# One pair of reciprocal-root operations for two samples, a moved send, and a reordered drain in a three-layer attention and expert kernel

## Chip, cores and metric

One core of one Trainium2 chip. The metric is the device time of one execution in microseconds (us); lower is better. The kernel before was timed three times: median 1148.78 us, from 1148.51 to 1149.47.

## The reference, cut to what matters

The input is 16 samples of 256 tokens with 128 features. Three layers follow one another, each a causal attention with 16 heads of width 8 behind a layer norm:

```
x = x + LN(attn0(LN(x)))                       # phase 0
f = LN(x)
f = f + attn1(LN(f));  h = LN(f)                # phase 1
f = f + token_moe(h)    # each token: its top 2 of 8 experts, gelu FFN 128-512-128
f = f + attn2(LN(f));  h = LN(f)                # phase 2
f = f + seq_moe(h)      # each sample: top 2 of 8 experts, from the mean of h
x = x + LN(f)
```

Each LN here is `(x - mean) / sqrt(var + 1e-5)`, followed by a scale and shift where the layer has one.

## The kernel before, in words

**Items, steps and slots.** A sample in a phase is an item with a number v: v = 0 to 15 is phase 0, 16 to 31 is phase 1 ("phase two" in the name of the change), 32 to 47 is phase 2. The kernel works through a software pipeline by steps n, and each step has four slots k = 0 to 3, one for each group of four heads. In step n the attention scores of item n are made; items n+1 and n+2 (`nxt`, `nxt2`) are prepared; items n-1 to n-5 (`old`, `older`, `oldest`, `first`, and one more) are finished. The order on each engine is written out by hand in one function per engine: `pe_slot`, `act_slot`, `dve_slot`, `pool_slot`, `sp_slot`. A run of such steps covers v = 0 to 31, so that its last steps (n = 32 and on) only finish old items: the drain. Then the token experts run (`pe_jobs` and its fellows), then a second run of steps for v = 32 to 47, then the experts of whole samples.

**The reciprocal roots.** Two layer norms per step need 1/sqrt(var + eps). VectorE (DVE) makes the moments: `post_mv` of item n-2 (`dve_residual_moments`) and `pre_mv` of item n+2, both in slot 2, on either side of the second row-maximum (`dve_reduce`, L616). GpSimd (POOL) makes the roots in `pool_rstd`, an addition (L891) and a power with exponent -0.5 (L893), each over 128 x 2 elements: once for `post_r` at the head of slot 2, and once for `pre_r` between the two causal selects of that slot (`pool_select`, L900). DVE then normalises: `hn` in slot 2 after the third row-maximum (`dve_normalise`, L662), `xn` in slot 3 (L662 too).

**The routed rows.** For each phase-1 item, DVE finds the top two experts of every token (`dve_top`) and the place of each token in its expert's list (`dve_place`, pieces 0 to 5; piece 5, L780, writes the row numbers `x_at`). GpSimd then sends the normalised rows `hk` to `x_routed` in DRAM with four indirect DMAs per item (`pool_send`, L925): send 0 in slot 3 of step v+4, sends 1, 2 and 3 in slots 0, 1 and 2 of step v+5. Piece 5 of item v waits until the sends of item v-2 have landed, because `x_at` has two buffers. Send 0 waits for piece 5 of its item. In slot 3, after its two selects, GpSimd also adds the output bias to `f_all` (`pool_bias`, L953).

**The end of the first run.** When item 31 is counted, `dve_tables` builds the list of expert jobs in 27 small DVE operations, each waiting for the one before; after the 18th (L1093) SyncE and ScalarE write zero padding behind each expert's rows (`pads`, L1359), and SyncE loads the first jobs (L1368) once padding and all sends have landed. TensorE (PE) starts on the jobs when the first rows are there (L1281). `dve_tables` begins by waiting for all seven increments of item 31's placing:

```
dve.wait_ge(placed, NPLACE * B)
```

In `dve_slot` the drain keeps the order of full steps: the normalisation of item n-2 comes ahead of `dve_top(oldest, 0)` (L732).

Of the kernel before, what the change touches and what calls it, by code (L numbers as in the profile page):

```python
# [7 lines left out]
ALU = mybir.AluOpType  # L8
# [7 lines left out]
P = 128  # L16
# [3 lines left out]
NG = H // HG  # L20
E = 8
TOP = 2
EPS = 1e-5
# [9 lines left out]
NPRE, NRSTD, NRES, NSPLIT = 4, 4, 14, 3  # L33
STACK_DMAS = TERMS
NTOP, NPLACE = 5, 7


def need(eng, sem, value):

    if isinstance(value, int) and value <= 0:  # L40
        return
    eng.wait_ge(sem, value)


def build(nc, x_in, w_qk, w_v, w_o, b_qk, b_v, b_o, ln1, ln2, gate_w, gate_b, e_w1, e_b1, e_w2, e_b2, out):
    B, T, D = x_in.shape
# [10 lines left out]
    pe, act, dve, pool, sp = nc.tensor, nc.scalar, nc.vector, nc.gpsimd, nc.sync  # L57

    with ExitStack() as ctx:
        def sb(name, shape, dt=F32):  # L60
            return ctx.enter_context(nc.sbuf_tensor(name, shape, dt))

        def sem(name):
            return ctx.enter_context(nc.semaphore(name))
# [34 lines left out]
        power = sb("power", [P, 2])  # L99
# [3 lines left out]
        pre_mv = sb("pre_mv", [P, 2, 2, 2])  # L103
        pre_r = sb("pre_r", [P, 2, 2])
# [20 lines left out]
        post_mv = sb("post_mv", [P, 2, 2, 2])  # L125
        post_r = sb("post_r", [P, 2, 2])
        st2 = sb("st2", [P, 2, 6])
        mv2 = sb("mv2", [P, 2, 2, 2])
# [68 lines left out]
        res, post_rstd = sem("res"), sem("post_rstd")  # L197
# [486 lines left out]

        def dve_residual_stats(i):
            src = tiles(f_all, i) if i.phase > 0 else [att[:, i.par, j] for j in range(2)]
            dve_stats(src, post_st, res, summed(i))

        def dve_residual_moments(i):
            need(dve, post_rstd, NRSTD * (i.v - 2) + 2)  # L690
            dve_moments(post_st, post_mv[:, i.par], res, summed(i))

        def dve_normalise(i):

            dve.wait_ge(post_rstd, NRSTD * i.v + (2 if i.phase == 0 else NRSTD))
            if i.phase > 0:
                need(dve, hT_ps, i.v - B - 1)
                if i.phase == 1:
                    need(dve, hk_sb, i.v - B - 1)
                dve_normal([hn[:, i.par, j] for j in range(2)], tiles(f_all, i), post_mv[:, i.par],  # L700
                           post_r[:, i.par], res, NRES - 7)
            else:
                att_j = [att[:, i.par, j] for j in range(2)]
                dve_normal(att_j, att_j, post_mv[:, i.par], post_r[:, i.par], res)
# [6 lines left out]
        def dve_f(i):  # L711

            dve.wait_ge(post_rstd, NRSTD * i.v + NRSTD)
            dve_normal(tiles(f_all, i), tiles(x_all, i), mv2[:, i.par], r2[:, i.par], res)
# [104 lines left out]
        def dve_slot(step, k):  # L819
# [51 lines left out]
            if k == 1 and nxt2 and nxt2.phase == 2:  # L871
                dve_combine(nxt2, 1)
            if k == 2 and older:
                dve_normalise(older)
            if k == 2 and ranked:
                dve_top(oldest, 0)
# [4 lines left out]
            if k == 3 and placing:  # L881
                dve_place(first, 5)
            if k == 3 and older and older.phase == 0:
                need(dve, post_rstd, NRSTD * (older.v - 2) + 4)
                dve_moments(st2, mv2[:, older.par], res, NRES * older.v + 8)


        def pool_rstd(mv, r, s, base, last=1):

            alone(pool)  # L890
            nc.gpsimd.tensor_scalar(r, mv[:, :, 1], EPS, None, ALU.add).then_inc(s, 1)  # L891
            pool.wait_ge(s, base + 1)
            nc.gpsimd.tensor_tensor(r, r, power[:], ALU.pow).then_inc(s, last)  # L893
# [62 lines left out]
        def pool_slot(step, k):  # L956
# [4 lines left out]
            if k == 2 and older:  # L961
                pool.wait_ge(res, summed(older) + 4)
                pool_rstd(post_mv[:, older.par], post_r[:, older.par], post_rstd, NRSTD * older.v,
                          1 if older.phase == 0 else NRSTD - 1)
            if k == 0 and oldest and oldest.phase == 0:
                pool.wait_ge(res, NRES * oldest.v + 12)
                pool_rstd(mv2[:, oldest.par], r2[:, oldest.par], post_rstd, NRSTD * oldest.v + 2)
            if ie:
                pool_select(ie, ge, 0)
            if k == 2 and nxt2:  # L970
                pool.wait_ge(pre_stats, NPRE * nxt2.v + 4)
                need(pool, xn_ok, 2 * (nxt2.v - 2) + 2)
                pool_rstd(pre_mv[:, nxt2.par], pre_r[:, nxt2.par], pre_rstd, 2 * nxt2.v)
# [14 lines left out]
            if sending and sending.phase == 1:  # L988
                pool_send(sending, (k + 1) % NG)
# [56 lines left out]
        def dve_tables():  # L1046
# [15 lines left out]
            dve.wait_ge(placed, NPLACE * B)  # L1062
# [17 lines left out]
            step(nc.vector.tensor_reduce(mask, t, AX.X, ALU.add))  # L1080
            step(nc.vector.tensor_tensor(t, t, starts, ALU.mult))
# [17 lines left out]
            flat = [a[:].rearrange("p t r -> p (t r)") for a in (expert_all, place_all, y_at_all)]  # L1099
            step(nc.vector.tensor_copy(t, flat[0].unsqueeze(2).to_broadcast([P, NT * TOP, E])))  # L1100
# [636 lines left out]
```

## Time and profile before

| | |
|---|---|
| median of three runs | 1148.78 us |
| the profiled execution | 1144.85 us, its span 1143.1 us |
| PE busy | 1012.9 us, 89% of the span |
| DVE busy | 875.4 us, 77% |
| ACT (ScalarE) busy | 773.9 us, 68% |
| POOL busy | 703.0 us, 61% |
| GpSimd sends, L925 | 64, mean 1017 ns |
| GpSimd selects, L900 | 384, mean 647 ns |

The span is what the hardware profiler recorded of one execution on the core; the execution's own time is a little longer, since launch and end lie around it. Busy shares are means over stages with different limits. A row of a timeline reads: start in us from the start of the span, duration in us (of all its instructions together, where it ends in x2 or more), engine, line and operation, output and input tile, and in brackets how long the engine was idle before and what released it.

### The profile page before, as it was taken

To read this page: it belongs to the slowest core of one execution; us is meant where nothing else is said; L and a number is where in the kernel's file an instruction comes from. 1 tells how busy PE (TensorE), PEld (TensorE's weight loads), DVE (VectorE), ACT (ScalarE), POOL (GpSimd) and SP (SyncE) were. 2 spreads that over 40 slices of the span, in tenths; PEclk is the share of its full clock that TensorE was granted. 3 is DMA by queue.
4 is the path that set the end of the run, shared out by engine and by line. 5 is a ranking of instruction groups with operands and counts; after the bars stand their busy time and mean duration, and the time that the engine had idled before them with its cause. 6 is when DMAs were issued, how large, how long until landed. Compare 5 with 4: busy or idle time off the path is not lost.

```text
span 1143.1 us, 34934 instructions
## 1 busy us (share of the span) xinstructions
PE 1012.9 (89%) x10453; PEld 789.0 (69%) x10453; DVE 875.4 (77%) x2669; ACT 773.9 (68%) x1913; POOL 703.0 (61%) x1050
## 2 busy tenths in 40 slices
PE   3799999999999999998189999189999999989996
PEld 2566677666677766765189999156666666669986
DVE  5699999999989888887645555178899889856665
ACT  2677777777777777776067778157777777655554
POOL 3466666666667888887623332667888887433331
PEclk8999999999999999999589999589999999999999
DMA  5343212222212222221122222244322222100000
GB/s 159 107 120 82 55 51 56 54 53 56 52 51 63 65 67 67 68 66 37 56 59 70 71 67 63 69 126 124 91 67 70 69 63 61 44 2 15 20 19 24
DMA packets 120711, 73.73 MB, mean 64 GB/s; under 512 B 10736, under 2 KB 115568, under 8 KB 120560
## 3 DMA queue, kind: packets, MB, share of 16 engines
q1 hardware_dynamic: 101552, 51.59, 16.7%
q10 hardware_dynamic: 14912, 11.88, 3.7%
q0 software_dynamic: 4096, 8.40, 2.6%
q8 instruction: 77, 1.26, 0.5%
q14 instruction: 74, 0.61, 0.2%
HBM read 21.68 MB, written 11.60 MB: 29 GB/s over the span
## 4 chain that ended last, share of the span: by engine, by line
PE 31%; DVE 7%; issue 5%; POOL 3%; DMA 3%; ACT 2%; SPq 1%; POOLq 0%; DVEq 0%; ACTq 0%
PE bank L1220 10%; PE bank L1209 9%; DVE wide L616 3%; PE bank L348 2%; DMA stack<-mT 2%; PE bank L393 1%; POOL y_got L944 1%; PE bank L315 1%; PE bank L375 1%; PE bank L334 1%; DVE f_all L795 1%; PE bank L311 1%; ACT prob L503 1%; PE bank L1281 1%; PE bank L381 1%
## 5 line engine op out<-in xcount | busy, mean ns | idle before, releaser
L616 DVE TENSOR_REDUCE wide<-bank 128x2 f32<-128x512 f32 (+1 forms) x576 | 388.7, 678 | 83.7 <-PE bank L307 68.5
L503 ACT ACTIVATE prob<-bank 128x512 f32<-128x512 f32 x576 | 336.8, 592 | 84.8 <-PE bank L329 66.2
L900 POOL TENSOR_SCALAR_AFFINE_SELECT prob<-prob 128x512 f32<-128x512 f32 x384 | 246.1, 647 | 95.5 <-ACT prob L503 93.8
L348 PE MATMUL bank<-prob,vaug 128*32 128x256 f32 (+1 forms) x3072 | 165.3, 333 | 5.2 <-issue 3.9
L1240 POOL COPY w_job<-w_s 128x512 f32 x104 | 66.0, 635 | 154.2 <-PE bank L1209 153.5
L315 PE MATMUL bank<-stack 126*128 126x256 bf16 x768 | 147.8, 273 | 0.0
L334 PE MATMUL bank<-stack 128*128 128x256 bf16 x768 | 146.8, 272 | 0.9 <-ACT prob L503 0.9
L1220 PE MATMUL bank<-w_job,prob 128*128 128x128 f32 x1088 | 139.0, 276 | 1.9 <-issue 1.6
L1231 ACT ACTIVATE prob<-bank,b_job 128x128 f32<-128x128 f32 (+1 forms) x416 | 132.0, 400 | 8.6 <-PE bank L1209 7.8
L348 PEld LDWEIGHTS bank<-prob,vaug 128*32 128x32 f32 x3072 | 81.5, 109 | 78.6 <-issue 46.6
L1220 PEld LDWEIGHTS bank<-w_job,prob 128*128 128x128 f32 x1088 | 131.3, 192 | 5.5 <-issue 4.5
L311 PE MATMUL bank<-maskneg,identb 128*128 128x256 bf16 x384 | 105.7, 275 | 5.5 <-DVE wide L616 4.6
L329 PE MATMUL bank<-stack 128*128 128x128 bf16 x768 | 75.1, 220 | 19.3 <-DMA stack<-mT 18.3
L514 ACT COPY mT<-bank 8x256 bf16<-8x256 bf16 x192 | 67.8, 353 | 33.3 <-PE bank L359 33.1
L925 POOL DMA_INDIRECT x_routed<-hk,x_at x64 | 65.1, 1017 | 28.0 <-DVE x_at L780 11.1
L334 PEld LDWEIGHTS bank<-stack 128*128 128x128 bf16 x768 | 73.3, 97 | 12.4 <-ACT prob L503 1.8
L315 PEld LDWEIGHTS bank<-stack 126*128 126x128 bf16 x768 | 75.8, 99 | 6.4 <-issue 0.6
L305 PE MATMUL bank<-maskneg,identb 128*128 128x512 bf16 x192 | 74.0, 385 | 6.1 <-DMA stack<-parts 4.6
L944 POOL DMA_INDIRECT y_got<-y_routed,y_at x64 | 63.8, 997 | 25.0 <-POOL y_at L941 12.2
L1209 PE MATMUL bank<-oT,w_job 128*128 128x128 f32 x576 | 77.5, 278 | 0.0
L307 PEld LDWEIGHTS bank<-stack 126*128 126x128 bf16 x768 | 59.9, 98 | 24.8 <-issue 1.1
L625 DVE TENSOR_TENSOR wide<-wide 128x8 bf16<-128x8 f32 x192 | 71.6, 373 | 6.6
(186 smaller groups left out, 2029.4 us busy)
## 6 DMA issues: line engine op xcount, KB each, us to landing
stack<-parts SPq DMA_DIRECT2D x576, 64.0 KB
w_s<-e_w ACTq DMA_DIRECT2D x32, 256.0 KB, 3.1
oT<-x_routed SPq DMA_DIRECT2D x72, 64.0 KB, 1.8
y_routed<-oT SPq DMA_DIRECT2D x36, 128.0 KB, 1.9
stack<-mT SPq DMA_DIRECT2D x192, 4.0 KB
out<-x_all SPq DMA_DIRECT2D x16, 128.0 KB, 1.8
b_all<-e_b ACTq DMA_DIRECT2D x2, 512.0 KB, 4.0
x_routed<-hk,x_at POOLq DMA_INDIRECT x64, 2.3
```

The source lines that it names most:

```text
L311: nc.tensor.matmul(o[:, :, P:T], identb[:], maskneg[:, 0:2], start=True, stop=False, skip_group_check=True)
L315: m = nc.tensor.matmul(o[:, h], q[:, hh, P:T], k[:, hh, :], start=False, stop=True, skip_group_check=True)
L329: m = nc.tensor.matmul(bk[:, h * P:(h + 1) * P], k[:, p0 + h, P:T], q[:, p0 + h, P:T], start=True, stop=True)
L334: m = nc.tensor.matmul(bk[:, h * T:(h + 1) * T], k[:, hh, 0:P], q[:, hh, :], start=True, stop=True)
L348: m = nc.tensor.matmul(o, w, (prob0, prob1)[kb][:, g % 2, h], start=kb == 0, stop=kb == 1, skip_group_check=True)
L503: nc.scalar.activation(o, s, ACT.Exp, scale=SCALE).then_inc(exp_done, 1)
L616: nc.vector.tensor_reduce(o, s, AX.X, ALU.max, negate=True).then_inc(max_done, 1)
L900: nc.gpsimd.affine_select(out=t, in_=t, compare_op=ALU.is_ge, fill=0.0, base=0, pattern=[[0, HG], [1, P]], channel_multiplier=-1).then_inc ...
L944: nc.gpsimd.indirect_dma_start(y_got[:, i.par, t, rank], None, y_routed, bass.IndirectOffsetOnAxis(ap=y_at[:, i.par, t, rank:rank + 1], ax ...
L1209: m = nc.tensor.matmul(bank[2 * par + c // 2][:, (c % 2) * T:(c % 2) * T + width], w1_job[:, par, c * P:(c + 1) * P], rows, start=True, st ...
L1220: m = nc.tensor.matmul(y_bank[par][:, t * P:(t + 1) * P], hid[:, par, c, t * P:(t + 1) * P], w2_job[:, par, c], start=(c == 0), stop=(c == ...
L1231: nc.scalar.activation(hid[:, par, c, 0:width], bank[2 * par + c // 2][:, (c % 2) * T:(c % 2) * T + width], ACT.Gelu, bias=b1_job[:, par, ...
```

## The change

Three edits:

- **Roots of two samples together.** For items v with 16 <= v < 28 (`joint`), the roots of item n-2 (`post_r`) and item n+2 (`pre_r`) are one addition and one power over 128 x 4 elements, at the head of slot 2, once both moments are there; the pair between the two selects is gone. That holds for steps n = 18 to 29. The tiles `pre_mv`, `post_mv` and `pre_r`, `post_r` become halves of common tiles, `power` has four columns. The semaphores are counted anew (`post_ready`, `x_rstd`).
- **Sends.** While `nxt2` exists (n < 30 in the first run), send 2 moves from slot 1 to slot 2, where send 3 follows it. After that the sends keep their slots.
- **Drain.** In steps without a current item `dve_top(oldest, 0)` comes ahead of `dve_normalise(older)`. `dve_tables` waits only for the counts (piece 2) of item 31; piece 5 of item 31 moves from slot 3 into the tables, behind their eighth operation (L1080).

```diff
-        power = sb("power", [P, 2])
+        power = sb("power", [P, 4])
-        pre_mv = sb("pre_mv", [P, 2, 2, 2])
-        pre_r = sb("pre_r", [P, 2, 2])
+        pre_post_mv, pre_post_r = sb("pre_post_mv", [P, 2, 2, 2, 2]), sb("pre_post_r", [P, 2, 2, 2])
+        (pre_mv, post_mv), (pre_r, post_r) = ([a[:, :, kind] for kind in range(2)] for a in (pre_post_mv, pre_post_r))
...
+        def joint(v):
+            return B <= v and v + 4 < 2 * B
+        separate = [v for v in range(3 * B) if not joint(v)]
+        def post_ready(v):
+            return (pre_rstd, 2 * (v + 4) + 2) if joint(v) else (post_rstd, 2 * separate.index(v) + 2)
...
         def dve_normalise(i):
-            dve.wait_ge(post_rstd, NRSTD * i.v + (2 if i.phase == 0 else NRSTD))
+            dve.wait_ge(*post_ready(i.v))
...
+            if k == 2 and ranked and not cur:
+                dve_top(oldest, 0)
             if k == 2 and older:
                 dve_normalise(older)
-            if k == 2 and ranked:
+            if k == 2 and ranked and cur:
                 dve_top(oldest, 0)
...
-            if k == 3 and placing:
+            if k == 3 and placing and first.v < 2 * B - 1:
                 dve_place(first, 5)
...
-        def pool_rstd(mv, r, s, base, last=1):
+        def pool_rstd(mv, r, s, base):
...
-            nc.gpsimd.tensor_tensor(r, r, power[:], ALU.pow).then_inc(s, last)
+            exponents = power[:, 0:2] if len(r.shape) == 2 else power[:].rearrange("p (a b) -> p a b", a=2)
+            nc.gpsimd.tensor_tensor(r, r, exponents, ALU.pow).then_inc(s, 1)
+        def pool_pre(i, mv, r):
+            pool.wait_ge(pre_stats, NPRE * i.v + 4)
+            need(pool, xn_ok, 2 * (i.v - 2) + 2)
+            pool_rstd(mv[:, i.par], r[:, i.par], pre_rstd, 2 * i.v)
...
             if k == 2 and older:
                 pool.wait_ge(res, summed(older) + 4)
-                pool_rstd(post_mv[:, older.par], post_r[:, older.par], post_rstd, NRSTD * older.v,
-                          1 if older.phase == 0 else NRSTD - 1)
+                if joint(older.v):
+                    pool_pre(nxt2, pre_post_mv, pre_post_r)
+                else:
+                    pool_rstd(post_mv[:, older.par], post_r[:, older.par], post_rstd, post_ready(older.v)[1] - 2)
...
-            if k == 2 and nxt2:
-                pool.wait_ge(pre_stats, NPRE * nxt2.v + 4)
-                need(pool, xn_ok, 2 * (nxt2.v - 2) + 2)
-                pool_rstd(pre_mv[:, nxt2.par], pre_r[:, nxt2.par], pre_rstd, 2 * nxt2.v)
+            if k == 2 and nxt2 and not (older and joint(older.v)):
+                pool_pre(nxt2, pre_mv, pre_r)
...
             if sending and sending.phase == 1:
-                pool_send(sending, (k + 1) % NG)
+                for n in (((1,), (2,), (3,), (0,)) if not nxt2 else ((1,), (), (2, 3), (0,)))[k]:
+                    pool_send(sending, n)
...
         def dve_tables():
-            dve.wait_ge(placed, NPLACE * B)
+            dve.wait_ge(placed, NPLACE * B - NPLACE + 4)
...
             step(nc.vector.tensor_reduce(mask, t, AX.X, ALU.add))
+            dve_place(Item(2 * B - 1, 1, 1), 5)
             step(nc.vector.tensor_tensor(t, t, starts, ALU.mult))
...
+            dve.wait_ge(placed, NPLACE * B)
             step(nc.vector.tensor_copy(t, flat[0].unsqueeze(2).to_broadcast([P, NT * TOP, E])))
```

## Rows read from the trace of the kernel before

**Rows 1.** Busy time in a stretch of phase 1: PE, PEld, DVE, ACT, POOL, clock, DMA share, GB/s

```profile
410.00:451.00 41.00, 39.21 (x450) 28.38 (x449) 36.52 (x125) 30.78 (x71) 35.52 (x53) 1.00 0.25 68
```

**Rows 2.** Waits of PE from 343 to 510 us: total, times, longest

```profile
PE bank L400 <- DVE on L635: 3.6, 9, 0.4
```

**Rows 3.** Timeline of POOL in step 22, end of slot 1 to slot 3

```profile
377.52 0.98 POOL L925 DMA_INDIRECT x_routed<-hk,x_at  x1 [0.15 <-issue]
378.54 0.24 POOL L891 TENSOR_SCALAR post_r<-post_mv 128x2 f32<-128x2 f32 x1
378.94 0.72 POOL L893 TENSOR_TENSOR post_r<-post_r,power 128x2 f32<-128x2 f32 x1 [0.15 <-POOL post_r L891]
...
380.25 0.21 POOL L891 TENSOR_SCALAR pre_r<-pre_mv 128x2 f32<-128x2 f32 x1
380.54 0.71 POOL L893 TENSOR_TENSOR pre_r<-pre_r,power 128x2 f32<-128x2 f32 x1
...
382.02 1.11 POOL L925 DMA_INDIRECT x_routed<-hk,x_at  x1 [0.17 <-issue]
...
384.35 0.72 POOL L953 TENSOR_TENSOR f_all<-f_all,bo_s 128x256 f32<-128x256 f32 x1
```

**Rows 4.** Timeline of DVE in the same step

```profile
378.28 0.24 DVE L651 BATCH_NORM_AGGREGATE pre_mv<-pre_st 128x2 f32<-128x6 f32 x2
...
379.70 0.91 DVE L662 TENSOR_SCALAR hn<-f_all,post_mv,post_r 128x128 f32<-128x128 f32 x2 [0.31 <-POOL post_r L893]
...
384.58 0.53 DVE L625 TENSOR_TENSOR wide<-wide 128x8 bf16<-128x8 f32 x1
```

**Rows 5.** Timeline of PE: the stall after step 22 and after step 30

```profile
386.63 0.44 PE L400 MATMUL bank<-ident,on 128*128 128x128 f32 x2 [0.39 <-DVE on L635]
...
519.23 0.44 PE L400 MATMUL bank<-ident,on 128*128 128x128 f32 x2 [0.90 <-DVE on L635]
```

**Rows 6.** Timeline of POOL in step 30: two selects in a row, and the bias

```profile
512.83 1.21 POOL L900 TENSOR_SCALAR_AFFINE_SELECT prob<-prob 128x512 f32<-128x512 f32 x2
...
517.03 0.73 POOL L953 TENSOR_TENSOR f_all<-f_all,bo_s 128x256 f32<-128x256 f32 x1
```

**Rows 7.** Timeline of DVE in step 30

```profile
512.88 1.24 DVE L662 TENSOR_SCALAR hn<-f_all,post_mv,post_r 128x128 f32<-128x128 f32 x2 [0.83 <-POOL post_r L893]
```

**Rows 8.** Timeline of DVE in step 20: moments that an idle POOL waits for

```profile
344.42 0.23 DVE L651 BATCH_NORM_AGGREGATE post_mv<-post_st 128x2 f32<-128x6 f32 x2
```

**Rows 9.** Timeline of POOL in step 20

```profile
344.85 0.22 POOL L891 TENSOR_SCALAR post_r<-post_mv 128x2 f32<-128x2 f32 x1 [0.84 <-DVE post_mv L651]
```

**Rows 10.** Groups of POOL instructions by shape, whole execution: busy us, mean ns

```profile
L909 POOL TENSOR_TENSOR rest<-qkf,parts 128x512 f32<-128x512 f32 x48 | 55.8, 1163 | 18.6 <-ACT parts L524 14.9 <-issue 0.4
...
L953 POOL TENSOR_TENSOR f_all<-f_all,bo_s 128x256 f32<-128x256 f32 x32 | 23.2, 725 | 0.0
```

**Rows 11.** Timeline of DVE in the drain

```profile
549.12 0.60 DVE L662 TENSOR_SCALAR hn<-f_all,post_mv,post_r 128x128 f32<-128x128 f32 x2 [1.43 <-POOL post_r L893]
549.63 0.23 DVE L732 MAX8 mx_all<-lgt 128x8 f32<-128x8 f32 x2
...
555.83 0.19 DVE L776 TENSOR_REDUCE place_all<-picked 128x4 f32<-128x32 f32 x1
558.29 0.16 DVE L780 SCALAR_TENSOR_TENSOR x_at<-expert_all,place_all 128x4 uint32<-128x4 f32 x1 [2.28 <-DMA x_routed<-hk,x_at]
...
562.12 0.76 DVE L1081 TENSOR_TENSOR prob<-prob,js 128x576 f32<-128x576 f32 x1
```

**Rows 12.** Timeline of POOL in the drain: a send right behind another, and the last

```profile
546.98 0.96 POOL L925 DMA_INDIRECT x_routed<-hk,x_at  x1 [0.30 <-issue]
...
566.88 1.14 POOL L925 DMA_INDIRECT x_routed<-hk,x_at  x1 [0.30 <-issue]
```

**Rows 13.** The chain of waits, in order of time: landing of sends, padding, first job

```profile
555.92 2.27 DMA x_routed<-hk,x_at
...
570.09 1.74 DMA x_routed<-zeros
```

More of the change, by code:

```diff
@@ L32 @@
 SPREAD = 4
-NPRE, NRSTD, NRES, NSPLIT = 4, 4, 14, 3
+NPRE, NRES, NSPLIT = 4, 14, 3
 STACK_DMAS = TERMS
@@ L124, in build @@
         post_st = sb("post_st", [P, 2, 6])
-        post_mv = sb("post_mv", [P, 2, 2, 2])
-        post_r = sb("post_r", [P, 2, 2])
         st2 = sb("st2", [P, 2, 6])
@@ L196, in build @@
         o1_ps, attn_n, o2_ps, onT_sb, o3_ps = sem("o1_ps"), sem("attn_n"), sem("o2_ps"), sem("onT_sb"), sem("o3_ps")
-        res, post_rstd = sem("res"), sem("post_rstd")
+        res, post_rstd, x_rstd = sem("res"), sem("post_rstd"), sem("x_rstd")
         hT_ps, hT_sb, lg_ps, lg_sb = sem("hT_ps"), sem("hT_sb"), sem("lg_ps"), sem("lg_sb")
@@ L689, in dve_residual_moments @@
         def dve_residual_moments(i):
-            need(dve, post_rstd, NRSTD * (i.v - 2) + 2)
+            if i.v >= 2:
+                dve.wait_ge(*post_ready(i.v - 2))
             dve_moments(post_st, post_mv[:, i.par], res, summed(i))
         def dve_normalise(i):
-            dve.wait_ge(post_rstd, NRSTD * i.v + (2 if i.phase == 0 else NRSTD))
+            dve.wait_ge(*post_ready(i.v))
             if i.phase > 0:
@@ L711, in dve_f @@
         def dve_f(i):
-            dve.wait_ge(post_rstd, NRSTD * i.v + NRSTD)
+            dve.wait_ge(x_rstd, 2 * i.v + 2)
             dve_normal(tiles(f_all, i), tiles(x_all, i), mv2[:, i.par], r2[:, i.par], res)
@@ L880, in dve_slot @@
                 dve_place(first, 4)
-            if k == 3 and placing:
+            if k == 3 and placing and first.v < 2 * B - 1:
                 dve_place(first, 5)
             if k == 3 and older and older.phase == 0:
-                need(dve, post_rstd, NRSTD * (older.v - 2) + 4)
+                need(dve, x_rstd, 2 * (older.v - 2) + 2)
                 dve_moments(st2, mv2[:, older.par], res, NRES * older.v + 8)
-        def pool_rstd(mv, r, s, base, last=1):
+        def pool_rstd(mv, r, s, base):
             alone(pool)
-            nc.gpsimd.tensor_scalar(r, mv[:, :, 1], EPS, None, ALU.add).then_inc(s, 1)
+            nc.gpsimd.tensor_scalar(r, mv[..., 1], EPS, None, ALU.add).then_inc(s, 1)
             pool.wait_ge(s, base + 1)
-            nc.gpsimd.tensor_tensor(r, r, power[:], ALU.pow).then_inc(s, last)
+            exponents = power[:, 0:2] if len(r.shape) == 2 else power[:].rearrange("p (a b) -> p a b", a=2)
[4 more added lines that the diff above has]
+            pool_rstd(mv[:, i.par], r[:, i.par], pre_rstd, 2 * i.v)
         def pool_select(i, g, u):
@@ L962, in pool_slot @@
                 pool.wait_ge(res, summed(older) + 4)
-                pool_rstd(post_mv[:, older.par], post_r[:, older.par], post_rstd, NRSTD * older.v,
-                          1 if older.phase == 0 else NRSTD - 1)
+                if joint(older.v):
+                    pool_pre(nxt2, pre_post_mv, pre_post_r)
+                else:
+                    pool_rstd(post_mv[:, older.par], post_r[:, older.par], post_rstd, post_ready(older.v)[1] - 2)
             if k == 0 and oldest and oldest.phase == 0:
                 pool.wait_ge(res, NRES * oldest.v + 12)
-                pool_rstd(mv2[:, oldest.par], r2[:, oldest.par], post_rstd, NRSTD * oldest.v + 2)
+                pool_rstd(mv2[:, oldest.par], r2[:, oldest.par], x_rstd, 2 * oldest.v)
             if ie:
                 pool_select(ie, ge, 0)
-            if k == 2 and nxt2:
-                pool.wait_ge(pre_stats, NPRE * nxt2.v + 4)
-                need(pool, xn_ok, 2 * (nxt2.v - 2) + 2)
-                pool_rstd(pre_mv[:, nxt2.par], pre_r[:, nxt2.par], pre_rstd, 2 * nxt2.v)
+            if k == 2 and nxt2 and not (older and joint(older.v)):
+                pool_pre(nxt2, pre_mv, pre_r)
             if k == 1 and nxt:
```

## Prediction

> **What bounds the kernel now.** First the busy time by stretch. In phase 1 PE is busy 39.21 of 41 us at full clock [rows 1]: it bounds these steps, and only time in which it stands still can be won. Then PE's waits there: they put nine stalls, 3.6 us together, ahead of the transposes of L400, each waiting for DVE's `on` [rows 2]; one of them is the 0.39 us at 386.63 [rows 5]. The count fits steps 21 to 29, the joint steps in which sends run. A step takes about 16.6 us there (519.23 less 386.63, over eight steps [rows 5]).
>
> Then the timelines, to see who makes DVE late. In slot 2 DVE idles 0.31 us for `post_r` ahead of `hn` [rows 4], which comes late because send 2 sits ahead of it on GpSimd and ends where L891 starts [rows 3]. But this is not yet what sets PE's stall. In slot 3 DVE's L625, over 8 elements, takes 0.53 us and ends at 385.11, just after GpSimd's bias (384.35 and 0.72, to 385.07) [rows 3, 4]: it is held until the bias is done. From the bias's end to L400 is 1.56 us in this step. In step 30 the bias ends at 517.76 and L400 starts at 519.23, 1.47 us later [rows 5, 6], though DVE had idled 0.83 us for its roots there [rows 7]. So the chain is GpSimd up to its bias, then DVE, then PE, and **what counts is when GpSimd ends its slot 3**, not how long DVE waits in slot 2.
>
> At the end of the first run another chain holds: sends of item 29 land, piece 5 of item 31, the tables, the padding, the first job [rows 11, 13].
>
> **Part 1, one pair of roots (12 steps).** It removes the second pair: 0.21 and 0.71 us, from 380.25 to 381.25, less 0.03 by which the next select overlaps: -0.97 us of GpSimd [rows 3]. The joint pair must wait for `pre_mv`, which ends at 378.52 [rows 4]. An idle GpSimd starts 0.20 us after such moments (344.65 to 344.85) [rows 8, 9], so at 378.72 instead of 378.54 [rows 3]: +0.18 us. DVE's wait ahead of `hn` gets no shorter by that, it grows to about 0.5 us. Behind the pair the two selects now follow one another, as in step 30, where the two operations of `hn`, begun beside them, took 1.24 us [rows 6, 7] against 0.91 us now [rows 4]; in exchange `xn` has no select beside it. Both lie in DVE's time before it is held by the bias, so I cost them at nothing; if that cover goes they are worth about 0.3 us each way.
>
> No row shows a power over four elements. Below, it costs as much as over two (+0). Above, all that the power adds doubles: L909 over 512 elements takes 1163 ns and L953 over 256 takes 725 [rows 10], which extrapolates to some 0.29 us for a very small two-input operation, so of 0.72 us [rows 3] 0.43 us belong to two powers, and two more cost +0.43. I take +0.2, about the middle, since no row lies nearer to either end. A gain is excluded: it is the same operation on more data.
>
> The Trainium skill (GPSIMD Engine Reference, section 3.1) puts two-input GpSimd operations at about 2.6 cycles for each element of a partition, by which two more elements would be nearly free. The power row, with its 0.43 us over the extrapolated add, speaks for a dearer element; by the page alone the term would be 0, which is a rival below.
>
> **Part 2, the send.** Send 2 leaves slot 1 (0.98 us [rows 3]). That frees nothing: GpSimd would be waiting for `pre_mv` there anyway, since the send ends at 378.50. In slot 2 it comes behind the selects and send 3 follows it: one send of 0.98 us [rows 3] and the 0.30 us that lies between two sends in a row [rows 12], +1.28 us. The send there now takes 1.11 us [rows 3], beside `xn`; up to 0.1 us may come back.
>
> Sum for GpSimd's slot 3: +0.18 - 0.97 + 1.28 = +0.49, less 0.1, so **+0.4 us, and +0.6 with the power**. It passes the selects of slot 3, the bias, L625, `x_at`, `on` and L400, whose stall grows from 0.4 to about 1.0 us. Send 0 waits for `x_at` and moves with it. Nine steps: +5.4 us. In steps 18 to 20 no send runs in slot 2, the pair removed outweighs the later start, and GpSimd comes to slot 3 before its data: 0. Steps 30 and 31 are unchanged.
>
> **Part 3, the drain.** `x_at` of item 31 waits 2.28 us for the sends of item 29, and the tables start right behind it, at about 558.5; the operation ahead of it ends at 556.02 [rows 11]. The tables can start then: -2.45 us. Their ninth operation starts at 562.12, 3.6 us after the first [rows 11], so piece 5 in its new place comes at about 559.7, later than the landing at 558.19 [rows 13], so it waits no more and costs its own 0.2 us: +0.2. `dve_top` moved ahead lies in DVE's idle time (1.43 us before `hn`), and the most of its 0.23 us leaves the chain, in step 32 and again in step 33 [rows 11]; I estimate that 0.15 us of it reaches the tables, since from step 34 TensorE's and ScalarE's work on the last item's `hn` leads. Together **-2.4 us**.
>
> What is late next: the last send starts at 566.88 [rows 12] and a send lands 2.27 us after its start [rows 13], at 569.15, some 0.3 us sooner with the drain's earlier start. The padding lands at 571.83 [rows 13], and -2.4 makes it 569.4. So the gain just fits; the sends are 0.2 to 0.6 us behind taking over.
>
> **Sum.** +5.4 - 2.4 = **+3.0 us**. The profiled execution took 1144.85 us (span 1143.1), 3.9 us below the median of 1148.78; I add to the median: **1151.8 us**. A difference of 0.2%, 2.3 us, is about what a measurement of this kernel can tell from no change.
>
> **Rivals.**
> - *The power over four costs no more than over two* (or the send gives more back). Then nine steps cost 9 x 0.4 = 3.6 us, less 2.4: **+1.2, 1150.0 us**, no change. For it: an addition over 2 elements takes 0.21 to 0.24 us [rows 3], so most of a small operation is fixed. Against: the power's 0.43 us above.
> - *Faster: DVE gets past the bias.* With `xn` free of a select (about 0.3 us sooner) L625 may start before GpSimd's later bias does. It decides if DVE reaches L625 after the last select and before the bias; then GpSimd is no longer ahead of `on`, DVE's own queue is, and the stall of 0.39 us shrinks by some 0.2: -1.8 - 2.4 = **-4.2, 1144.6 us**. Against: in step 30 the interval from bias to L400 held although DVE stood otherwise, and the next small operations would be held in L625's place.
> - *The drain gives nothing*, because indirect sends beside the earlier tables run longer (1.14 us against 0.96 [rows 12]) and land last, with those of item 31 behind a later `x_at`. Then **+5.4, 1154.2 us**. Against: `x_at` comes at 559.9, its send in about 563.
>
> The Trainium skill (SBUF — State Buffer, "Who interferes with whom") says that a fast-mode VectorE copy or scalar operation and GpSimd lock one another out of a port pair, descriptor writing included. Of that the send of 1.11 us beside `xn` shows 0.13 us; by the rule two sends beside `xn` could be held by up to its whole length, which would lie on the slower side of my sum.
>
> **How the numbers follow.** Forecast 0.44, power free 0.26, DVE past the bias 0.22, drain gives nothing 0.08. With the power at its upper bound the forecast ends at 9 x 0.83 - 2.4 = +5.1. Low end 1144.5 (the faster rival), high end 1154.3. Forecast's own range: 1150 to 1154; a sixth of it is below +2.3. Slower: 0.37 + 0.08 = 0.45; same: 0.26 + 0.07 = 0.33; faster 0.22.
>
> **What would show it.** Right: steps 21 to 29 at about 17.2 us; L400's wait some 1.0 us each, still 1.5 us behind the bias's end; `hn` pairs of 1.2 us behind a wait of 0.5 to 0.7; the power over 128x4 at about 0.9 us; the tables' first operation some 2.5 us sooner after item 31's last `hn`; the padding still landing last. Wrong: a power at 0.72 (rival one), L400's wait at 0.4 or less with L625 short again (rival two), SyncE's first job waiting for a send (rival three).

## The result, and the profile after

The changed kernel takes **1152.96 us** (median of 11 runs, 1150.23 to 1156.62); the kernel before, run beside it, 1148.51 us (11 runs, 1144.83 to 1150.14). The ratio is 1.0043, 95% interval 1.0031 to 1.0055: slower by 4.9 us, between 3.6 and 6.3. The forecast was 1151.8 us, 3.0 above its base, in a range of 1144.5 to 1154.3.

The profiled execution of the changed kernel took 1156.49 us, span 1154.8, so it was one of its longest; its span is 11.7 us above the one of before. Not all of that is the change: of the 11.5 us by which its last GpSimd `rest` (L927; L909 before) is late, 2.3 were there before the first joint step and 2.3 more come in the middle of the second run, where nothing was changed. (The other traces stand there, ahead of the first joint step, between 0.9 us ahead and 2.7 behind; and all four traces of the third occasion below, e10 and e11 without joint roots among them, show the same long step of about 19 us in the second run.) So the steps are read from this profile and, where ends matter, from a second profile of the same kernel (run `e8_changed_again`, span 1146.7 us), in which `rest` stood 0.1 us *ahead* of before when the joint steps began. Lines have moved: L393 is now L391, L400 L398, L616 L614, L625 L623, L635 L633, L651 L649, L662 L660, L780 L789, L891 and L893 are L902 and L905, L900 L918, L925 L943, L953 L971, L1281 L1302, L1359 L1380. In e3 and e4 GpSimd's lines stand two lower (L903, L916, L969).

The page's busy time, to set beside the table of before: every engine is as busy as it was, or less.

```profile
PE 1012.7 (88%) x10358; PEld 789.7 (68%) x10453; DVE 869.9 (75%) x2669; ACT 774.0 (67%) x1913; POOL 698.6 (60%) x1026
```

Phase 1 by stretch, as in [rows 1] (PE, PEld, DVE, ACT, POOL, clock, DMA share, GB/s). GpSimd is busy 2.9 us less in it. The same clock times cut the steps elsewhere, though; over eight whole steps, from `rest` to `rest` (377.79 to 515.65; before 373.62 to 506.80), it is 108.76 us for 113.75, 0.62 less a step. And yet the steps are longer:

```profile
410.00:451.00 41.00, 38.92 (x445) 27.77 (x446) 34.61 (x114) 30.29 (x72) 32.62 (x43) 1.00 0.23 65
```

Next the timeline of GpSimd over slots 2 and 3 of a joint step, to be read against [rows 3]:

```profile
417.33 0.23 POOL L902 TENSOR_SCALAR pre_post_r<-pre_post_mv 128x4 f32<-128x4 f32 x1 [1.33 <-DVE pre_post_mv L649]
417.64 1.05 POOL L905 TENSOR_TENSOR pre_post_r<-pre_post_r,power 128x4 f32<-128x4 f32 x1
418.68 1.22 POOL L918 TENSOR_SCALAR_AFFINE_SELECT prob<-prob 128x512 f32<-128x512 f32 x2
420.08 1.09 POOL L943 DMA_INDIRECT x_routed<-hk,x_at  x1 [0.18 <-issue]
421.47 0.96 POOL L943 DMA_INDIRECT x_routed<-hk,x_at  x1 [0.30 <-issue]
422.45 1.23 POOL L918 TENSOR_SCALAR_AFFINE_SELECT prob<-prob 128x512 f32<-128x512 f32 x2
423.64 0.72 POOL L971 TENSOR_TENSOR f_all<-f_all,bo_s 128x256 f32<-128x256 f32 x1
```

And DVE in the same stretch, against [rows 4]:

```profile
416.90 0.24 DVE L649 BATCH_NORM_AGGREGATE pre_post_mv<-pre_st 128x2 f32<-128x6 f32 x2
...
418.73 1.25 DVE L660 TENSOR_SCALAR hn<-f_all,pre_post_mv,pre_post_r 128x128 f32<-128x128 f32 x2 [0.72 <-POOL pre_post_r L905]
...
420.63 0.62 DVE L660 TENSOR_SCALAR xn<-f_all,pre_post_mv,pre_post_r 128x128 f32<-128x128 f32 x2
...
423.35 0.40 DVE L623 TENSOR_TENSOR wide<-wide 128x8 bf16<-128x8 f32 x1
423.67 0.73 DVE L750 CAST expert_all<-mi 128x4 f32<-128x4 uint32 x1
```

The joint addition starts 0.19 us behind the second moments (417.14 to 417.33). The power takes 1.05 us, `hn` waits 0.72 us and then takes 1.25, `xn` only 0.62. Two sends stand behind the two selects, 0.30 us apart. The bias ends at 424.36, which is 7.22 us after the moments of `pre_mv`; before it was 6.55 (378.52 to 385.07 [rows 3, 4]): 0.67 us later. DVE's cast L750 ends with it, at 424.40, then come the row numbers and `on`, and PE's L398 starts at 425.84:

```profile
425.84 0.44 PE L398 MATMUL bank<-ident,on 128*128 128x128 f32 x2
```

Where PE stands still for it differs from one execution to the next. In the second profile it waits at L398 in all nine steps; in the profile of the result at L398 for DVE in two only, and in five ahead of L373, for ScalarE's `xT` (1.2 us), though its steps are as long. First the second profile, PE's waits from 343 to 515 us (total, times, longest), against [rows 2]:

```profile
PE bank L398 <- DVE on L633: 4.5, 9, 0.5
PE bank L309 <- DVE wide L614: 3.0, 10, 0.3
PE bank L391 <- ACT oT L507: 2.7, 10, 0.3
```

Two of PE's transposes there, seven steps apart:

```profile
388.98 0.44 PE L398 MATMUL bank<-ident,on 128*128 128x128 f32 x2 [0.51 <-DVE on L633]
...
509.51 0.44 PE L398 MATMUL bank<-ident,on 128*128 128x128 f32 x2 [0.50 <-DVE on L633]
```

A step takes 120.53 / 7 = **17.22 us**; before it was 16.65 from one `rest` to the next (132.60 / 8 = 16.58 by [rows 5], which take in step 30). The old stall grew only from 0.4 to 0.5 us. The same count in the profile of the result:

```profile
PE bank L398 <- DVE on L633: 0.7, 2, 0.4
```

The second wait is new: ten times 0.3 us ahead of L309, the matmul of the mask, released by a row maximum of DVE (L614), in both profiles. This stall is already there in the first joint steps, where the old one was not and no send runs in slot 2 (PE, profile of the result):

```profile
336.01 0.28 PE L309 MATMUL bank<-maskneg,identb 128*128 128x256 bf16 x1 [0.29 <-DVE wide L614]
...
352.49 0.28 PE L309 MATMUL bank<-maskneg,identb 128*128 128x256 bf16 x1 [0.30 <-DVE wide L614]
...
420.77 0.28 PE L309 MATMUL bank<-maskneg,identb 128*128 128x256 bf16 x1 [0.30 <-DVE wide L614]
```

Over exactly those steps the windows show PE idle 8.39 us of seven steps, 1.20 each; in the kernel before, from 386.63 to 519.23, 132.60 - 126.24 = 6.36 us of eight, 0.80 each:

```profile
388.98:509.51 120.53, 112.14 (x1260) 80.45 (x1275) 103.50 (x337) 88.95 (x205) 95.07 (x127) 1.00 0.23 64
```

That would be 0.40 of the 0.6 us, as much as 0.1 at L398 and 0.3 at L309. But this count is rough, since some matmul records are missing: e1 below, whose steps are those of the kernel before, shows 1.00 us of idle a step over six steps. So PE's idle time doesn't say how much is lost where.

What does is the distance from the end of `pre_mv`'s moments (L649) to the start of L398, in us, in the settled steps, where it repeats within some 0.02 us from step to step. The kernels e3 to e9 are those of the experiments below:

| kernel | `pre_mv` to end of bias | `pre_mv` to L398 | step | step less `pre_mv` to L398 |
|---|---|---|---|---|
| before | 6.55 | 8.11 | 16.65 | 8.54 |
| e3 joint roots only | 6.59 | 8.19 | 16.73 | 8.54 |
| e4 moved send only | 6.87 | 8.05 | 16.59 | 8.54 |
| e9 send and drain | 6.89 | 8.06 | 16.60 | 8.54 |
| the change (result) | 7.22 | 8.70 | 17.23 | 8.53 |
| the change (e8) | 7.20 | 8.68 | 17.22 | 8.54 |
| e6 change, bias late | 9.84 | 8.07 | 16.67 | 8.60 |
| e7 send, drain, bias late | 9.36 | 7.58 | 16.20 | 8.62 |

All that the step gains or loses lies between these two points (the last column stays within 0.1; e10 has 8.01 and 8.48, e11 8.17 and 8.60), also in the profile in which PE hardly waits at L398. In the change the bias ends 0.65 to 0.67 us later, and L398 comes 0.57 to 0.59 later with it.

The drain's timeline of DVE in that profile: the tables begin at 561.99, and piece 5 of item 31 follows 3.5 us later without a wait; before it had waited 2.28 us, ahead of the tables [rows 11].

```profile
561.99 0.28 DVE L1084 COPY prob<-counts 128x256 f32<-128x256 f32 x1
...
565.50 0.16 DVE L789 SCALAR_TENSOR_TENSOR x_at<-expert_all,place_all 128x4 uint32<-128x4 f32 x1
```

At the 32nd `rest`, behind the last of the joint steps, it was 6.35 us behind before; its tables start 3.50 us later, its first job 3.64 us later (578.67 against 575.03). So the drain gives back 2.7 us there. What the first job now waits for is the last send. The chain of waits, in order of time, against [rows 13], and SyncE's padding beside it, issued from 570.14 to 573.79:

```profile
572.95 2.53 DMA x_routed<-hk,x_at
...
577.84 1.93 DMA oT<-x_routed
```

```profile
570.14 3.65 SPq L1380 DMA_DIRECT2D x_routed<-zeros  x4
```

In the profile of the result it is otherwise. It is 8.85 us behind at the 32nd `rest` and 6.31 at the tables (564.80), 2.5 less, but 8.71 at the first job (583.74): only 0.1 us is given back. The paddings took longer, and the last of them landed at 580.46, behind the sends, of which the last started at 574.51:

```profile
573.49 5.77 SPq L1380 DMA_DIRECT2D x_routed<-zeros  x4
```

### The profile page after: what moved, and what is told of

Same layout as the page of the kernel before. It is cut to its first block, busy times and chain, and to the rows that moved or that the text cites. A ratio compares the mean times of both kernels' runs of the same rounds, so it can differ in the third digit from the quotient of the medians.

```text
span 1154.8 us, 34784 instructions
## 1 busy us (share of the span) xinstructions
PE 1012.7 (88%) x10358; PEld 789.7 (68%) x10453; DVE 869.9 (75%) x2669; ACT 774.0 (67%) x1913; POOL 698.6 (60%) x1026
## 4 chain that ended last, share of the span: by engine, by line
PE 59%; DVE 12%; issue 11%; DMA 7%; POOL 5%; ACT 4%; SPq 1%; DVEq 0%; POOLq 0%; ACTq 0%
PE bank L1241 10%; PE bank L1230 9%; PE bank L346 8%; DMA stack<-mT 5%; PE bank L313 4%; DVE wide L614 4%; PE bank L332 4%; PE bank L373 3%; PE bank L391 3%; PE bank L305 2%; PE bank L309 2%; PE bank L404 2%; PE bank L327 2%; PE bank L365 2%; PE bank L379 1%
## 5 line engine op out<-in xcount | busy, mean ns | idle before, releaser
L614 DVE TENSOR_REDUCE wide<-bank 128x2 f32<-128x512 f32 (+1 forms) x576 | 389.0, 679 | 94.8 <-PE bank L305 70.3
L918 POOL TENSOR_SCALAR_AFFINE_SELECT prob<-prob 128x512 f32<-128x512 f32 x384 | 246.4, 649 | 99.1 <-ACT prob L501 97.1
L309 PE MATMUL bank<-maskneg,identb 128*128 128x256 bf16 x384 | 106.2, 277 | 11.7 <-DVE wide L614 10.8
L305 PE MATMUL bank<-stack 126*128 126x128 bf16 x768 | 75.1, 220 | 10.8 <-DMA stack<-parts 3.6
L943 POOL DMA_INDIRECT x_routed<-hk,x_at x64 | 64.7, 1012 | 28.1 <-issue 10.9
L507 ACT COPY oT<-bank 128x256 f32<-128x256 f32 x192 | 69.8, 364 | 7.4 <-PE bank L346 6.1
```

Source lines behind the costliest of these rows:

```text
L305: m = nc.tensor.matmul(o[:, h], q[:, p0 + h, 0:P], k[:, p0 + h, 0:P], start=False, stop=True, skip_group_check=True)
L309: nc.tensor.matmul(o[:, :, P:T], identb[:], maskneg[:, 0:2], start=True, stop=False, skip_group_check=True)
L614: nc.vector.tensor_reduce(o, s, AX.X, ALU.max, negate=True).then_inc(max_done, 1)
L918: nc.gpsimd.affine_select(out=t, in_=t, compare_op=ALU.is_ge, fill=0.0, base=0, pattern=[[0, HG], [1, P]], channel_multiplier=-1).then_inc ...
```

## The experiments

All kernels compute the full result. Each was timed in five rounds beside the kernel before. They ran on three occasions (the first and the third on one chip, the second on another), on which the kernel before took 1144.62 us (24 runs), 1145.48 (17) and 1148.62 (31); ratios are compared within an occasion first. The ratio stands with its 95% interval. The step is the mean of the last six before the drain, from one `rest` to the next; in the kernel before it is 16.65 us.

| run | occasion | median us | ratio to before | step us |
|---|---|---|---|---|
| e1 drain only | 1 | 1140.95 | 0.9970 [0.9955, 0.9985] | 16.61 |
| e2 steps only | 1 | 1150.61 | 1.0045 [1.0032, 1.0059] | 17.24 |
| e3 joint roots only | 1 | 1148.45 | 1.0031 [1.0018, 1.0043] | 16.73 |
| e4 moved send only | 1 | 1143.18 | 0.9981 [0.9967, 0.9995] | 16.59 |
| e8 the change again | 2 | 1150.55 | 1.0043 [1.0028, 1.0058] | 17.22 |
| e9 send and drain | 2 | 1142.02 | 0.9963 [0.9948, 0.9977] | 16.60 |
| e6 change, bias late | 2 | 1147.38 | 1.0016 [1.0002, 1.0030] | 16.67 |
| e7 send, drain, bias late | 2 | 1139.54 | 0.9945 [0.9927, 0.9962] | 16.20 |
| e12 the change, third time | 3 | 1151.98 | 1.0033 [1.0020, 1.0047] | 17.23 |
| e13 steps only again | 3 | 1154.35 | 1.0050 [1.0034, 1.0067] | 17.24 |
| e10 as e7, first run only | 3 | 1146.46 | 0.9982 [0.9966, 0.9997] | 16.49 |
| e11 as e10, send in slot 1 | 3 | 1148.55 | 0.9998 [0.9983, 1.0014] | 16.77 |

**The halves of the change.** Steps and drain taken apart. The edits are to the changed kernel. e1 takes back joint roots and send:

```diff
-            return B <= v and v + 4 < 2 * B
+            return False
...
-                for n in (((1,), (2,), (3,), (0,)) if not nxt2 else ((1,), (), (2, 3), (0,)))[k]:
+                for n in ((1,), (2,), (3,), (0,))[k]:
```

> The drain's edits alone; roots and sends as before. Theory: the tables start 2.5 us sooner behind the last steps, padding and first job come 2.4 us sooner, ratio to before 0.998. Rival: the padding beside the last sends is issued more slowly (5.7 us for SyncE's four instead of 3.6, as the profile of the changed kernel shows), so the tables are sooner by 2.6 us and the first job by under 0.5 us; ratio 1.000. Steps 21 to 29 stay at 16.65 us in both.

e2 takes back the drain, and e13 is the same kernel once more:

```diff
-            if k == 2 and ranked and not cur:
-                dve_top(oldest, 0)
...
-            if k == 2 and ranked and cur:
+            if k == 2 and ranked:
...
-            if k == 3 and placing and first.v < 2 * B - 1:
+            if k == 3 and placing:
...
-            dve.wait_ge(placed, NPLACE * B - NPLACE + 4)
+            dve.wait_ge(placed, NPLACE * B)
...
-            dve_place(Item(2 * B - 1, 1, 1), 5)
```

> Joint roots and moved send, drain as before. Theory: steps 21 to 29 take 17.2 us, the time rises by 5.5 to 7 us, ratio 1.005 to 1.006. Rival (the loss is from the new places of the tiles or is disturbance, since the profile also shows 1.5 us more near the start and 2.3 us near the end): steps at 16.65 to 16.8, ratio under 1.002.

The drain alone is 3.4 us faster by its ratio (1.7 to 5.2). In its trace the tables start at 556.20, before at 558.49, behind steps that are 0.3 us late by then, so 2.6 us sooner. The first job is 2.6 us sooner on the same count. In its chain of waits the last send comes last:

```profile
567.18 2.52 DMA x_routed<-hk,x_at
...
572.07 1.98 DMA oT<-x_routed
```

The steps alone are 5.2 us slower (3.7 to 6.8), with PE's waits as in the second profile of the change, to a tenth (L398 4.6 us in 9, L309 3.0 in 10). So the loss is in the steps, and the drain by itself does what it was forecast to do.

**The two edits of the steps apart.** e3 and e4 keep the old drain. e3 leaves the sends where they were (the second edit of e1), e4 keeps two pairs of roots (the first edit of e1).

> Joint roots, send 2 still in slot 1, drain as before. Theory (the end of GpSimd's bias in slot 3 sets the step): GpSimd loses the second pair (0.97 us) and adds 0.17 for the later start and 0.33 for the larger power, so the bias ends 0.5 us sooner than before, the steps take 16.5 to 16.7 us, change between -1.5 and +1 us, though VectorE waits 0.7 to 0.9 us for the roots. Rival (VectorE's wait ahead of hn sets the step): steps at 17.1 us or more, +4 to +6 us.

> Two sends in slot 2, separate roots, drain as before. Theory (bias): the bias ends about 0.35 us later than before, steps at about 17.0 us, +3 us, although VectorE no longer waits for its roots ahead of hn. Rival (VectorE's wait ahead of hn sets the step): that wait of 0.31 us is gone, steps at 16.35 us, -2.8 us.

Neither alone lengthens the settled step: +0.08 us with the joint roots, -0.06 with the moved send, **+0.58 with both**. The parts don't add up. The prediction had priced them as a bundle: it charged the moved send in full because, with joint roots, GpSimd would wait for `pre_mv` in the time that leaving slot 1 frees.

With the joint roots alone PE's waits from 343 to 515 us are only these. The 0.4 us at L400 are gone, and the 0.3 at L309 have taken their place:

```profile
PE bank L309 <- DVE wide L614: 3.0, 10, 0.3
PE bank L391 <- ACT oT L507: 2.7, 10, 0.3
```

DVE and GpSimd in e3: `hn` waits 0.84 us, and DVE comes to L623 at 422.55, when the bias, begun at 421.96, is all but over. Nothing is held. But the bias isn't 0.5 us sooner, as I had expected: it ends 6.59 us after `pre_mv`, before 6.55. GpSimd now waits for ScalarE's `prob` ahead of its selects (from 395 to 497 us 4.9 us in 12 waits, of a kind that doesn't stand among its waits before), so what it saved with the second pair is lost again; and DVE, late by `hn`, reaches L398's `on` no sooner either:

```profile
417.80 1.25 DVE L660 TENSOR_SCALAR hn<-f_all,pre_post_mv,pre_post_r 128x128 f32<-128x128 f32 x2 [0.84 <-POOL pre_post_r L903]
...
422.55 0.17 DVE L623 TENSOR_TENSOR wide<-wide 128x8 bf16<-128x8 f32 x1
422.67 0.17 DVE L750 CAST expert_all<-mi 128x4 f32<-128x4 uint32 x1
```

```profile
421.96 0.73 POOL L969 TENSOR_TENSOR f_all<-f_all,bo_s 128x256 f32<-128x256 f32 x1
```

The ratio of e3, 1.0031, is more than 0.08 us a step makes: its first four joint steps lose 1.7 us, so that the trace accounts for 2.3 of the 3.5 us (2.1 to 4.9). I had expected +1 us at most: the settled steps were as expected, the first four were not.

With the moved send alone the bias is late, as I expected of this run: it ends 0.3 us later against its step than before. But `hn` waits for nothing now, since no send stands ahead of its roots:

```profile
415.80 0.17 DVE L623 TENSOR_TENSOR wide<-wide 128x8 bf16<-128x8 f32 x1
415.92 1.32 DVE L750 CAST expert_all<-mi 128x4 f32<-128x4 uint32 x1
417.15 0.17 DVE L785 TENSOR_REDUCE place_all<-picked 128x4 f32<-128x32 f32 x1
417.36 0.52 DVE L789 SCALAR_TENSOR_TENSOR x_at<-expert_all,place_all 128x4 uint32<-128x4 f32 x1
...
428.37 0.60 DVE L660 TENSOR_SCALAR hn<-f_all,pre_post_mv,pre_post_r 128x128 f32<-128x128 f32 x2
```

```profile
415.92 1.24 POOL L916 TENSOR_SCALAR_AFFINE_SELECT prob<-prob 128x512 f32<-128x512 f32 x2
417.11 0.73 POOL L969 TENSOR_TENSOR f_all<-f_all,bo_s 128x256 f32<-128x256 f32 x1
```

DVE is early enough that L623 runs before the selects, the cast is held to their end (417.24 against 417.16) and L785 runs beside the bias. Only `x_at` is held to the bias's end, 417.88 against 417.84. So fewer operations are left behind the bias, and from its end to L398 it is 1.18 us, not 1.5: L398 comes 8.06 us after `pre_mv` as against 8.11 before. My rule "L400 is 1.5 us behind the bias" expected a slower kernel here; it is 2.2 us faster by its ratio (0.6 to 3.8). In its trace the first job comes 1.5 us sooner (573.56 against 575.03), of which 0.4 us was there before the first joint step. PE still waits at L398, and longer than before, since it gets there sooner:

```profile
PE bank L398 <- DVE on L633: 5.0, 9, 0.6
```

So the stall of L398 does not measure the loss: 0.40 us a step before, 0.56 here, 0.50 in the change, none in e3. The rule held in the changed kernel (424.36 to 425.84 is 1.48) only because DVE stands there as it did in steps 22 and 30.

**Is it the bias?** If the loss needs both a late DVE and a late bias, moving the bias behind send 0 and the copy of `hk` in slot 3 must take it away with both edits in. e8 is the changed kernel as it is, beside it. e9 takes the joint roots alone back out of the change (the first edit of e1). e6 is the changed kernel with

```diff
-            if k == 3 and nxt and nxt.phase > 0:
-                pool_bias(nxt)
...
                 nc.gpsimd.tensor_copy(hk[:, oldest.par], hn[:, oldest.par]).then_inc(hk_sb, 1)
+            if k == 3 and nxt and nxt.phase > 0:
+                pool_bias(nxt)
```

> The changed kernel itself, once more beside the others. Theory (the profile of it had a disturbed padding): SyncE's four paddings take 3.64 us as everywhere else, the first job comes about 6.3 - 2.6 = 3.7 us later than before, ratio about 1.003. Rival (roots, moved send and new drain together always lose the drain's gain): paddings take 5 us or more again, ratio 1.0045 or more. Steps 21 to 29 at 17.24 us in both.

> The changed kernel with GpSimd's bias moved behind send 0 and the copy of hk in slot 3. Theory (in the combination it is the bias that holds VectorE's row numbers, and the late hn is covered as in the kernel with joint roots alone): x_at is written about 0.5 us sooner, steps fall from 17.24 to 16.7 to 16.9 us, 3 to 5 us less than the changed kernel. Rival (the late hn and xn themselves set the step): steps stay at 17.1 us or more.

> The moved send and the new drain without the joint roots. If the parts add up: 0.9981 x 0.997, about -5 us, ratio 0.995 to 0.996. Rival (the drain's gain is taken by the sends, which here end at the same distance behind the steps): ratio 0.998. Steps at 16.55 to 16.6 us.

With the late bias the step goes from 17.22 to 16.67 us, `x_at` is written 6.90 us after `pre_mv` instead of 7.52 (e8), PE's waits at L398 vanish (9 times 0.5 in e8, none here) and L309 keeps its 2.9 us. An L623 of the next slot is now held, to the end of the two selects behind the bias (424.72 against 424.69), but PE waits nowhere for it:

```profile
422.80 0.73 POOL L971 TENSOR_TENSOR f_all<-f_all,bo_s 128x256 f32<-128x256 f32 x1
423.48 1.21 POOL L918 TENSOR_SCALAR_AFFINE_SELECT prob<-prob 128x512 f32<-128x512 f32 x2
```

```profile
420.16 0.15 DVE L750 CAST expert_all<-mi 128x4 f32<-128x4 uint32 x1
...
420.44 0.16 DVE L789 SCALAR_TENSOR_TENSOR x_at<-expert_all,place_all 128x4 uint32<-128x4 f32 x1
...
423.53 1.19 DVE L623 TENSOR_TENSOR wide<-wide 128x8 bf16<-128x8 f32 x1
```

Without the joint roots (e9) the step is 16.60. So the bias moved away or the joint roots taken out brings the step back, by 0.55 or 0.62 us. The 0.62 between e9 and e8 has two halves in the table above: the bias ends 0.31 us later (7.20 against 6.89), and behind its end it is another 0.31 longer to L398 (1.48 against 1.17), because DVE, late by `hn`, has more operations left. In the change, then, the bias holds DVE. That doesn't make the late `hn` harmless once the bias is gone: with the bias late in both, the joint roots still cost 0.47 us a step (e6 16.67, e7 16.20), and DVE comes to L623 6.2 us after `pre_mv` there, not 5.0. e9 is 4.2 us faster than before (2.6 to 6.0), a little less than the 2.2 of the moved send (e4) and the 3.4 of the drain (e1), as far as these intervals can tell. e8's own ratio, 1.0043, decides nothing between my theory of 1.003 and the rival of 1.0045 or more: its trace has the short paddings and the first job 3.7 us late, as the theory said, and its interval holds both.

**Versions with the late bias and separate roots.** e7 is e9 with the bias late; e10 is the same, but moves the bias in the first run alone, because e6 and e7 lose some 0.15 us a step in the second run by it (from `rest` to `rest` 16.35 us in e6, 16.19 in e8); e11 is e10 with the old place of send 2.

> Separate roots, moved send, new drain and the late bias. Theory (bias): x_at is free of the bias, the stall ahead of the transposes of on falls from 0.56 us to under 0.2, steps at 16.2 to 16.4 us, some 3 us less than with the send and the drain alone, ratio about 0.993. Rival (the bias in its new place holds VectorE's onehot and delays the selects and rest just as much): steps at 16.5 us or more.

> Separate roots, moved send, new drain, and the late bias in the first run only; in the second run the bias stays ahead of the fetches. Theory: steps 21 to 29 at 16.2 us as in the kernel with the late bias everywhere, and the 1.3 us that the second run lost there come back: ratio 0.993 to 0.994. Rival: the second run's loss has another cause, ratio 0.9945.

> As the kernel with the late bias in the first run, but send 2 back in slot 1. Theory: VectorE waits 0.3 us for its roots again, but GpSimd ends its slot 3 0.3 us sooner and nothing holds the row numbers: steps at 16.2 to 16.4 us, within 1.5 us of the other. Rival (the moved send is what matters): steps at 16.6 us.

e7 is the fastest kernel of the study: 1139.54 us, 6.3 us below before (4.4 to 8.4), on one occasion. Its steps take 16.20 us, and the only wait of PE for another engine that comes back in each is 0.3 us at L391. e10 and e11 missed. e10 has the same code in the steps of phase 1 as e7, but settled at 16.49, with another wait of PE:

```profile
PE bank L373 <- ACT xT L600: 3.2, 9, 0.7
PE bank L391 <- ACT oT L507: 2.8, 10, 0.3
```

Its ratio is 0.9982, and the expected second gain didn't show. Why the same order falls into one rhythm on one occasion and into another on the next is open; on the third occasion the four paddings of SyncE took 5.8 us in both e10 and e11, for 3.64 in e7, so the surroundings differed too: in e10's trace the tables come 2.9 us sooner behind the steps, the first job only 0.4. e11 against e10 says that the moved send is worth 0.28 us a step when the bias is out of the way. Whether 6.3 us is what e7 would give on any chip wasn't tried.

**The change, a third time.** To see if the changed kernel's difference hangs on the occasion, e12 (no edit) and e13 (e2's edit).

> The changed kernel beside the same kernel with the old drain, on one chip. Theory: in the trace the drain's gain of 2.6 us is there beside the joint roots too, so this one is 2 to 3 us below the other, ratio to before about 1.003. Rival: they are within 1 us of one another, and the drain's gain is given back somewhere behind the first job.

> Joint roots and moved send with the old drain, again. Theory: 6.3 to 6.7 us above before, ratio 1.0055. Rival: ratio 1.0043, the same as with the new drain.

The steps take 17.23 and 17.24 us, as on the other occasions, and the ratios are 1.0033 and 1.0050. The change is slower in all three comparisons. The drain is worth 1.9 us between these two (2.4 by the medians), but their intervals overlap, so that this difference alone isn't clear of noise. In e12's trace the paddings took 4.91 us and landed behind the last send; its tables come 2.8 us sooner behind the steps, its first job 1.4.

## Why the prediction was right, and where it was not

**The sign and the chain: right.** Slower, in the steps, through GpSimd's slot 3. Steps 21 to 29 were to take about 17.2 us; they take 17.23, 17.22, 17.23.

**The terms of GpSimd's sum: right.** The joint pair starts 0.2 us behind `pre_mv` (0.19). The power was costed at +0.2 between 0 and +0.43; it measured 1049 ns against 720 [rows 3], so +0.33, 0.13 above what I took. The groups by shape, whole execution, of the result's profile:

```profile
L905 POOL TENSOR_TENSOR pre_post_r<-pre_post_r,power 128x2 f32<-128x2 f32 x72 | 53.6, 745 | 6.1 <-ACT prob L501 0.2
...
L905 POOL TENSOR_TENSOR pre_post_r<-pre_post_r,power 128x4 f32<-128x4 f32 x12 | 12.6, 1049 | 1.0
```

Rival one (the power free) falls with this row. By the Trainium skill (GPSIMD Engine Reference, section 3.1), the two more elements should have cost next to nothing; measured, each costs some 0.16 us, so for a power the measurement decides against it. The send brought 0.96 + 0.30 for the forecast 1.28. The bias ends 0.67 us later for +0.6, and L398 0.57 to 0.59 later. For the settled steps the sum, the mechanism and the size are right.

**The stall: wrong.** "Whose stall grows from 0.4 to about 1.0 us" failed. L398 waits 0.5 us in e8 and mostly not at all in the profile of the result; 0.3 us a step are waited earlier, at L309, for DVE's row maximum, which the late and longer `hn` (0.72 and 1.25 us, both forecast) delays. That PE stands still there costs nothing more in the settled steps: e3 has the same 0.3 us and its step is 0.08 longer. I took PE's stall at one line for the measure of the loss; the distance from `pre_mv` to L398 is.

**Steps 18 to 20: wrong.** I costed them at 0 ("the pair removed outweighs the later start, and GpSimd comes to slot 3 before its data"). The first four steps of joint roots, 18 to 21, take 16.10, 16.45, 17.55 and 16.95 us from `rest` to `rest`, against 15.73, 15.84, 16.90 and 16.66 before: +1.9 us, 1.6 of them in steps 18 to 20. No send stands in the way in the first three, but GpSimd's first root now waits for the second moments, and `hn` with it. The step that failed is "Both lie in DVE's time before it is held by the bias, so I cost them at nothing": in the kernel before, PE waits ahead of L400 in none of these three steps, so there is no wait that takes up what it now stands still at L309. GpSimd doesn't come out sooner either: in slot 3 it waits for its data, and these come later, so that the bias ends 0.2 to 0.5 us later after `pre_mv` than before, and L398 comes 0.3 to 0.6 us later, 1.4 us together. e3 has the same four steps (16.09, 16.44, 17.55, 16.75), e4, without joint roots, has not (15.73, 15.76, 16.88, 16.40). Four stalls at L309, of 0.17 to 0.30 us, and one of 0.28 at L357 account for 1.3 us of it. The nine-step term was +5.4; steps 21 to 29 gave +5.0 (4.8 in e8).

**The rule of the bias: right for this kernel, wrong as a rule.** e4 has the late bias and its steps are no longer than before. The faster rival (DVE gets past the bias) was given 0.22. When the send moves alone L623 does get past it, but `x_at` is held in its place, as I had put against that rival, and the step is only 0.06 us shorter; in the change the joint roots make `hn` late, so DVE doesn't get past it. I named the condition of that rival and missed that one half of the change decides it for the other.

**The drain: right, where the paddings are as short as before.** -2.4 was forecast; traces show -2.6 (e1) and -2.7 (e8). The tie of sends and padding, forecast within 0.2 to 0.6 us, has gone to the sends in both, which costs little. But in the profile of the result and in e12 the paddings took 5.77 and 4.91 us instead of 3.64, landed last, and left 0.1 and 1.4 us of the gain. Rival three, by which the drain would give nothing because the sends land last, is refuted by e1; that slower paddings can take the gain stood in no rival, and what makes them slow is open.

**The sum.** In the second profile 6.4 us lost in steps and 2.7 given back make +3.7 (in the profile of the result 6.6 and 0.1: +6.5); the comparison says +4.9, from 3.6 to 6.3. The forecast of +3.0 lies below that interval. It was short by the 1.6 us of steps 18 to 20 and, in some executions, by what the paddings took from the drain; the nine steps had 0.4 to 0.6 too much. The Trainium skill (SBUF — State Buffer, "Who interferes with whom") says that a GpSimd operation and a fast-mode VectorE one lock each other out of their common port. The traces agree: the same cast takes 0.15 us behind the last select (e6) and 0.73 or 1.32 beside GpSimd (the change, e4), the pair of `hn` 0.60 without a select beside it (e4) and 1.25 beside two.

## What to carry to other kernels

Where two engines hold each other up through small locked operations, the cost of an edit depends on where the other engine stands: price a bundle of edits as a bundle, and split it on the chip (here +0.08 and -0.06 us a step alone, +0.58 together, and the send with the drain was faster by 0.37%). Don't take one engine's stall at one line for the loss: measure the distance between two fixed points of the step, and see if it moves as the step does. Joining two small operations saves a fixed cost but makes the earlier result wait for the later input: look at who needs the earlier one, even where it seems to have slack. A long operation of the helper engine (the bias) is best put where nobody waits for what it holds up: behind the send it held L623 for 1.19 us, and PE waited nowhere for that (e6). Which place that is changes with every move around it: with send 2 still in slot 1 the late bias gave steps of 16.77 us (e11), no better than the 16.65 before.

## What the runs showed of the hardware

- A GpSimd power costs 0.72 us over 128x2 and 1.05 us over 128x4: about 0.16 us for each further element of a partition; a fixed part of some 0.4 us is an estimate from these two rows.
- A DVE operation of 0.15 us can last 1.32 us: L750 in e4 is held for two GpSimd selects. It did not get in between these two, which run back to back; between the second select and the bias L623 did (0.40 us at 423.35, in the change), and L750 was held in its place.
- The same instruction order can run in two steady rhythms, 16.20 and 16.49 us a step (e7, e10). Four padding DMAs of SyncE take 3.64 or 3.65 us in one execution and 5.77 in another of the same kernel (e8, the result). I had expected neither, and the runs don't say what selects them.
